# State-space stage of an audio tower: softplus per chunk, means and the cap of the inverse decays on GpSimd

## The reference, cut to what matters

```python
delta = minimum(softplus(x_ssm @ delta_W + delta_b), 0.5)
A_cont = -exp(A_log)                      # (128, 16): 16 states
DeltaA = delta[..., None] * A_cont
A_bar = clip(exp(DeltaA), 0, 1)
injection = expm1(DeltaA) / A_cont
B_cont = silu(x_ssm @ B_W + B_b)          # per state
B_cont = 0.5 * (B_cont - mean(B_cont, axis=(0, 1)))
B_bar = injection * B_cont
A_shift = concatenate([ones, A_bar[:, :-1]], axis=1)
pps = exp(cumsum(log(maximum(A_shift, 1e-6)), axis=1))
h_seq = cumsum(B_bar * pps, axis=1) / pps
C_coeff = silu(x_ssm @ C_W + C_b)
h_out = einsum('btdn,btdn->btd', h_seq, C_coeff)
```

## Time and profile before

| | |
|---|---|
| time, median of 3 runs | 969.38 us (968.5 to 972.45) |
| the profiled execution: time / span | 968.98 / 967.2 us |
| VectorE busy | 676.2 us (70%) |
| TensorE matmul busy | 668.2 us (69%) |
| ScalarE busy | 488.4 us (51%) |
| GpSimd busy | 288.5 us (30%) |
| granted TensorE clock, mean | 0.829 |

### The profile page before, as it was taken

How to read it: one execution, slowest core, us unless ns; L and a number is a source line. 1 busy time by engine, 2 the same in 40 slices (tenths; PEclk the granted TensorE clock), 3 DMA queues, 4 the chain that set the end, 5 groups by cost and what they waited for, 6 DMA issues and landing times.

```text
span 967.2 us, 10956 instructions
## 1 busy us (share of the span) xinstructions
PE 668.2 (69%) x2944; PEld 497.5 (51%) x2945; DVE 676.2 (70%) x1490; ACT 488.4 (51%) x691; POOL 288.5 (30%) x266
## 2 busy tenths in 40 slices
PE   6974353753744646666531996469999999999996
PEld 3542253753744646533430775236666566566564
DVE  0987279999999999987850442656767676676651
ACT  1234799888988888803320332224434344343531
POOL 0443101000000000002684343133644537354352
PEclk9995576876778768789655998779999999999999
DMA  4300424543453345307011121100000000000000
GB/s 156 121 25 0 161 76 85 109 79 73 84 106 81 62 97 101 63 0 267 19 28 32 51 61 43 53 1 0 1 9 8 1 9 1 9 1 8 8 1 16
DMA packets 22519, 50.91 MB, mean 53 GB/s; under 512 B 4610, under 2 KB 14827, under 8 KB 22128
## 3 DMA queue, kind: packets, MB, share of 16 engines
q0 software_dynamic: 6752, 24.53, 13.0%
q1 hardware_dynamic: 15728, 25.92, 8.6%
HBM read 24.41 MB, written 10.10 MB: 36 GB/s over the span
## 4 chain that ended last, share of the span: by engine, by line
DVE 38%; PE 32%; issue 11%; POOL 7%; ACT 5%; POOLq 2%; DMA 2%; DVEq 1%; ACTq 0%; SPq 0%
PE psum L1715 6%; DVE s_R L1053 5%; DVE s_R L1048 5%; DVE s_R L1058 5%; PE psum L1774 4%; PE psum L1477 3%; POOL s_R L676 3%; PE psum L1644 3%; PE psum L1657 2%; DVE s_R L1027 2%; POOLq L178 2%; DVE s_R L1032 2%; POOL x_sorted L620 1%; DVE s_stat L203 1%; PE psum L1650 1%
## 5 line engine op out<-in xcount | busy, mean ns | idle before, releaser
L1538 PE MATMUL psum<-s_xn_lo,s_split_hi 128*128 128x368 f32 x256 | 101.4, 396 | 146.1 <-ACT s_R L785 97.6
L1538 PEld LDWEIGHTS psum<-s_xn_lo,s_split_hi 128*128 128x128 f32 x256 | 60.3, 236 | 151.7 <-ACT s_R L785 100.1
L1715 PE MATMUL psum<-s_R 128*128 128x368 f32 (+1 forms) x288 | 107.6, 499 | 0.3
L881 ACT ACTIVATE s_R<-psum,s_cols 128x368 f32<-128x368 f32 x96 | 52.6, 567 | 104.3 <-PE psum L1709 104.0
L1053 DVE TENSOR_TENSOR_SCAN s_R<-s_R 128x2944 f32<-128x2944 f32 x16 | 100.7, 6291 | 0.6
L1539 PE MATMUL psum<-s_xn_hi,s_split_lo 128*128 128x368 f32 x256 | 98.3, 384 | 0.0
L605 POOL DMA_DIRECT2D s_xnfm<-s_R x14 | 17.1, 1218 | 271.3 <-DVEq L1062 271.3
L1540 PE MATMUL psum<-s_xn_hi,s_split_hi 128*128 128x368 f32 x256 | 97.6, 381 | 0.0
L1707 PE MATMUL psum<-s_xn_lo,s_split_hi 128*128 128x368 f32 x144 | 75.0, 521 | 1.3 <-ACT s_R L881 1.3
L1715 PEld LDWEIGHTS psum<-s_R 128*128 128x128 f32 (+1 forms) x288 | 54.9, 200 | 30.9 <-issue 3.5
L666 POOL TENSOR_TENSOR s_R<-s_R 128x368 f32<-128x368 f32 x48 | 45.4, 946 | 74.8 <-DVE s_R L1331 71.8
(11 more groups left out here) (221 smaller groups left out, 1591.8 us busy)
## 6 DMA issues: line engine op xcount, KB each, us to landing
s_xnfm<-s_R POOLq DMA_DIRECT2D x14, 1472.0 KB, 10.5
s_R<-in_xg SPq DMA_DIRECT2D x8, 744.0 KB, 4.2
x_sorted<-in_x_init SPq DMA_DIRECT2D x1, 5082.0 KB, 19.3
s_R<-in_w SPq DMA_DIRECT2D x2, 1536.0 KB, 9.3
s_wBC<-in_wBC SPq DMA_DIRECT2D x8, 256.0 KB, 2.9
s_R<-x_sorted SPq DMA_DIRECT2D x28, 66.0 KB, 1.8
s_R<-y_rows SPq DMA_DIRECT2D x8, 184.0 KB
out<-s_R SPq DMA_DIRECT2D x8, 184.0 KB
```

Source lines behind the costliest of these rows:

```text
L1538: pe.matmul(bank(c), w_hi[:, s, u, k, :], xn_lo[:, a:b], start=True, stop=False)
L1715: ins = pe.matmul(bank((2, 4)[e % 2]), w, fh[0:kk, e % 3, j], start=(j == 0), stop=(j == FT - 1))
```

## The change

- The argument of delta is cut at ln(e^0.5 - 1), so that its softplus is cut at 0.5; the pass of VectorE that cut the result is gone. ScalarE takes exponential and logarithm per chunk (softplus), in its loop over pairs of chunks, which is written out; the table that holds both functions is loaded at the start. The stage boundary between stages 1 and 2 is gone, and waits on x_split, delta_mm, delta_read and delta_act stand where it stood.
- The weights of the first pair are loaded, copied and split during stage 1.
- The mean of B is made by GpSimd in three small operations (mean_of), which raise mean_ready.
- The cap of ra and its zeros are made by GpSimd (cap), which raises ra_capped. The cap of state n waits for ra_ready and for th_free of state n - 1, which the drive of state n - 1 raises; the scan of n - 1 is VectorE's next instruction.
- GpSimd's order in a pair is: cap of the even state, add_state of the odd state before, mean of the even state, cap and mean of the odd state, add_state of the even state.
- In the first pair ScalarE takes the silus of state 0 before the decays of state 1. On VectorE w_lo is made between scan and read-out, and the read-out raises its semaphore itself.

```diff
         def stage_end(eng, k):
             eng.drain().then_inc(stage_done, 1)
-            eng.wait_ge(stage_done, 4 * k)
+            eng.wait_ge(stage_done, 4 * (k - 1))
...
             sp.dma_start(prio[:, :], t["prio"]).then_inc(wload, 16)
+            sp.dma_start(wBC[:, :, :, :], t["wBC"][0]).then_inc(wBC_ready, 16)
...
             split_x(NP - 1)
-            stage_end(pool, 1)
+            pool.wait_ge(x_split, NCH)
+            pool.wait_ge(delta_mm, NCH)
             pool.memset(Y[:, :], 0.0).then_inc(Y_zero, 1)
             pool.wait_ge(Y_zero, 1)
-            def add_state(n, u):
-                wait_apart(pool, prod_ready, n + 1)
+            def add_state(n, u, first=False):
+                wait_apart(pool, prod_ready, n + 3)
+                if not first:
+                    wait_apart(pool, Y_added, 16 * n)
                 pool.dma_start(Y[:, :], bufC[:, u], accum_op=ALU.add, max_dma_last_dim=TOK // 2 * 4)\
                     .then_inc(Y_added, 16)
-                pool.wait_ge(Y_added, 16 * n + 16)
+            def mean_of(n, u):
+                wait_apart(pool, bc_free, NH + (n * 2 + 1) * NH)
+                wait_apart(pool, th_free, n + 1)
+                step.add(pool.tensor_tensor(part[:, u, 0:2], part[:, u, 0:2], part[:, u, 2:4], ALU.add))
+                step.wait()
+                step.add(pool.tensor_tensor(mean[:, u:u + 1], part[:, u, 0:1], part[:, u, 1:2], ALU.add))
+                step.wait(True)
+                pool.tensor_scalar(mean[:, u:u + 1], mean[:, u:u + 1], 1.0 / TOK, 0.0, ALU.mult, ALU.add)\
+                    .then_inc(mean_ready, 1)
+            def cap(n, u, scan=True):
+                if scan:
+                    wait_apart(pool, th_free, n + 2)
+                wait_apart(pool, ra_ready, n + 1)
+                pool.tensor_scalar(ra[:, u], ra[:, u], 1e6, 0.0, ALU.min, ALU.max).then_inc(ra_capped, 1)
+                wait_apart(pool, ra_capped, 2 * n + 1)
+                pool.memset(ra[:, u, 0:TOK:L], 0.0).then_inc(ra_capped, 1)
+            cap(0, 0, False)
+            mean_of(0, 0)
+            cap(1, 1)
+            mean_of(1, 1)
+            add_state(0, 0, True)
+            for i in step.loop(NPAIR - 2, 2 * 2):
+                cap(i * 2 + 2, 0)
+                add_state(i * 2 + 1, 1)
+                mean_of(i * 2 + 2, 0)
+                cap(i * 2 + 3, 1)
+                mean_of(i * 2 + 3, 1)
+                add_state(i * 2 + 2, 0)
...
+            act.preload_act_table_set("natural_log_exp_and_others")
...
+            def softplus(i):
+                for u in range(2):
+                    c = i * 2 + u
+                    d = dl[:, 1 + c * CT:1 + c * CT + CT]
+                    act.wait_ge(delta_read, 2 + c + 1)
+                    act.activation(d, d, ACT.Exp).then_inc(delta_act, 1)
+                    act.wait_ge(delta_act, 2 * c + 1)
+                    act.activation(d, d, ACT.Ln, bias=1.0, scale=1.0).then_inc(delta_act, 1)
...
-            act.activation(dl[:, 1:1 + TOK], dl[:, 1:1 + TOK], ACT.Exp).then_inc(delta_act, 1)
-            act.wait_ge(delta_act, 1)
-            act.activation(dl[:, 1:1 + TOK], dl[:, 1:1 + TOK], ACT.Ln, bias=1.0, scale=1.0).then_inc(delta_act, 1)
-            stage_end(act, 1)
+            weights_hi(0, 0)
+            for i in range(NP):
+                if i + 1 < NP:
+                    bias_copy(i + 1)
+                normed_twice(i)
+                if i:
+                    softplus(i - 1)
+                norms_fm(i)
             act.sem_inc(bc_free, NH)
+            softplus(NP - 1)
+            load_table(ACT.Tanh, 0)
+            act.wait_ge(delta_act, 2 * NCH)
...
-            weights_hi(0, 0)
-            decays(0)
+            tanh(0, 0)
+            exp_minus(0)
+            exp_plus(0, 0)
+            silus(0, (0,), True)
+            exp_plus(1, 1)
+            tanh(1, 1)
+            exp_minus(1)
             weights_hi(1, 1)
-            silus(0, True)
+            silus(0, (1,), True)
...
-                step.add(dve.tensor_scalar(ra[:, u], ra[:, u], 1e6, None, ALU.min))
-                step.wait()
-                step.add(dve.memset(ra[:, u, 0:TOK:L], 0.0))
...
             def drive(n, u):
-                dve.wait_ge(bc_free, NH + (n * 2 + 1) * NH)
-                step.add(dve.reduce_sum(mean[:, u:u + 1], part[:, u, :], axis=AX))
-                step.wait()
-                step.add(dve.tensor_scalar(mean[:, u:u + 1], mean[:, u:u + 1], 1.0 / TOK, None, ALU.mult))
-                step.wait()
+                dve.wait_ge(ea_free, n + 2)
+                dve.wait_ge(mean_ready, n + 1)
                 dve.scalar_tensor_tensor(bufB[:, u], bufB[:, u], mean[:, u:u + 1], th[:, u],
                                          ALU.subtract, ALU.mult).then_inc(th_free, 1)
             def recur(n, u):
+                dve.wait_ge(ra_capped, 2 * n + 2)
                 dve.wait_ge(th_free, 2 + n + 1)
                 dve.tensor_tensor_scan(bufB[:, u], ra[:, u], bufB[:, u], 0.0, ALU.mult, ALU.add).then_inc(ra_free, 1)
...
                 drive(n, 0)
                 recur(n, 0)
-                read_out(n, 0)
                 if weights:
                     weights_lo(i + 1, s)
+                read_out(n, 0)
                 drive(n + 1, 1)
                 recur(n + 1, 1)
                 if more:
                     injection(n + 2, 0)
-                    decay(n + 2, 0)
                 read_out(n + 1, 1)
                 if more:
                     injection(n + 3, 1)
-                    decay(n + 3, 1)
```

More of the change, by code:

```diff
@@ L605, in add_state @@
                 pool.dma_start(Y[:, :], bufC[:, u], accum_op=ALU.add, max_dma_last_dim=TOK // 2 * 4)\
                     .then_inc(Y_added, 16)
-                pool.wait_ge(Y_added, 16 * n + 16)
-            with pool.Fori(0, NPAIR - 1) as i:
-                for u in range(2):
-                    add_state(i * 2 + u, u)
+            def mean_of(n, u):
[7 more added lines that the diff above has]
+                    .then_inc(mean_ready, 1)
@@ L612, in _ @@
+            add_state(0, 0, True)
[6 more added lines that the diff above has]
+                add_state(i * 2 + 2, 0)
+            cap(NS - 2, 0)
+            add_state(NS - 3, 1)
+            mean_of(NS - 2, 0)
+            cap(NS - 1, 1)
+            mean_of(NS - 1, 1)
             stage_end(pool, 2)
@@ L733, in _, with weights_hi @@
+            def weights_hi(i, s):
+                act.wait_ge(wBC_ready, 16 * i + 16)
+                act.activation(w_hi[:, s], wBC[:, :, :, :], ACT.Copy).then_inc(w_hi_ready, 1)
             act.sem_inc(nA.xs1_ready, 2)
             bias_copy(0)
-            with act.Fori(1, NP) as i:
-                bias_copy(i)
-                norms_fm(i - 1)
-            norms_fm(NP - 1)
-            act.wait_ge(delta_read, 2 + NCH)
-            act.activation(dl[:, 1:1 + TOK], dl[:, 1:1 + TOK], ACT.Exp).then_inc(delta_act, 1)
@@ L773, in group, with silus @@
                 return tile[:, u, h * HB * CT:(h + 1) * HB * CT].rearrange("p (s n) -> p s n", s=HB)
-            def weights_hi(i, s):
-                act.wait_ge(wBC_ready, 16 * i + 16)
-                act.activation(w_hi[:, s], wBC[:, :, :, :], ACT.Copy).then_inc(w_hi_ready, 1)
-            def silus(i, first=False):
-                for u in range(2):
+            def silus(i, us=(0, 1), first=False):
+                for u in us:
                     n = i * 2 + u
-                    act.wait_ge(B_free, n + 1)
+                    act.wait_ge(prod_ready, n + 1)
                     for h in range(NH):
@@ L1013, in _ @@
             delta_arg(NP - 1)
-            dve.wait_ge(delta_act, 2)
-            step.add(dve.tensor_scalar(dl[:, 1:1 + TOK], dl[:, 1:1 + TOK], 0.5, None, ALU.min))
-            stage_end(dve, 1)
             dve.sem_inc(th_free, 2)
@@ L1057, in read_out @@
                 dve.wait_ge(bc_free, NH + (n * 2 + 2) * NH)
-                step.add(dve.scalar_tensor_tensor(bufC[:, u], bufB[:, u], A_c[:, bass.ds(n, 1)], bufC[:, u],
-                                                  ALU.mult, ALU.mult))
-                step.wait()
-                dve.sem_inc(B_free, 1)
-                dve.sem_inc(prod_ready, 1)
+                dve.scalar_tensor_tensor(bufC[:, u], bufB[:, u], A_c[:, bass.ds(n, 1)], bufC[:, u],
+                                         ALU.mult, ALU.mult).then_inc(prod_ready, 1)
             def pair(i, s, more=True, weights=True):
@@ L1078, in pair @@
                     injection(n + 3, 1)
-                    decay(n + 3, 1)
-            dve.sem_inc(w_split, 1)
-            weights_lo(0, 0)
             injection(0, 0)
-            decay(0, 0)
-            decay(1, 1)
+            drive(0, 0)
+            recur(0, 0)
+            read_out(0, 0)
             injection(1, 1)
-            pair(0, 1)
-            for i in step.loop(NPAIR // 2 - 1, 2 * (2 * 2 + 2 * 3)):
+            weights_lo(1, 1)
+            drive(1, 1)
+            recur(1, 1)
+            injection(2, 0)
```

(15 more changed lines are left out.)

55 lines of the change are left out of this document (28 added, 27 removed).

## The result

The changed kernel takes 978.44 us, median of 7 runs (973.89 to 980.46), beside 969.99 us for the kernel before (7 runs): a ratio of 1.008, interval 1.0059 to 1.0101. It is slower by 0.8%, where 986 was forecast, and a span of 978.6 us was profiled, in a run of 980.46 us.

What follows compares the result with a forecast made beforehand. VectorE was taken to bound the states' stage. To the profiled 968.98 us came +26 for seven pairs at +3.7 each and -9 for the earlier start, giving 986, with a range of 942 to 1008.

Steps and rivals of the forecast that it cites:

- The main step: States' stage: the scan, as one more two-input instruction, excludes the cap on GpSimd; +3.7 us a pair, +26 us in all.
- the memset of Y costed at nothing: Start of the stage: this memset on an idle GpSimd only writes, so it was put at no cost.
- a GpSimd instruction waits for a whole run of VectorE's, not for one: States' stage: the even cap waits out injection, read-out and injection to 9.7 us, then runs to 12.7.
- The even half: From odd scan to even scan: the drive starts at 15.0 us instead of 14.0 and ends at 18.3.
- The odd half: Even scan to odd scan: cap and zeroing 3.2, mean 0.8 behind the read-out; odd drive ends at 35.9 us.
- 4 us of idle: Sign that the forecast is right: VectorE idle this long before the odd drive, released by GpSimd's mean.
- The start: Softplus per chunk and no stage boundary: scan of state 1 at 140.8 against 150.82, 10 us ahead; -9 us net.
- ScalarE's late entry into the next pair: After the first pair: ScalarE comes late to the next one, which costs about 1 us.
- The first: Rival: the scan doesn't exclude GpSimd, or GpSimd slips in; 36.0 us a pair, 944 us; chance 0.28.
- The second: Rival: the cap costs like a two-input operation, +62 us, 1048; chance of a cap above 4.5 us 0.08.
- The third: Rival: exclusion, but caps fall partly in VectorE's waits, about half of the 3.7 us remains; 973 or 969; chance 0.09.
- The break-even of 39.5 us a pair: States' stage: a pair under this length, 38.2 + 9 / 7, makes the changed kernel faster than before.

Runs made afterwards that it cites:

- the fill: The changed kernel with GpSimd's cap replaced by a memset of 1.0 that only writes, at the same place with the same waits: 945.77 us.
- the last section: The changed kernel with long-fulfilled waits put between VectorE's seven products in the attention's stage, beside GpSimd's small power: 981.09 us.
- the best version: The changed kernel with the cap and the means both back on VectorE: 953.03 us, ratio 0.9829 to the kernel before.

## Why the prediction was right and wrong

**Right.** VectorE bounded the stage; without a cap the pair falls to 35.7 us (22.2 + 13.54), where 35.4 to 36 was worked out. The main step, that the scan is one more instruction that excludes a GpSimd read, holds: the cap of 8.48 us over a scan of 6.29, and the fill that isn't held. It was taken from differences and products and is now shown for the scan, beside which the cap, which reads, holds VectorE for 2.4 us and the fill, which only writes, doesn't (945.77 us). That it hangs on the two inputs of VectorE's instruction was the author's estimate: no run varies them beside the cap, and the last section has an instruction with one input that kept GpSimd out too. That a GpSimd instruction which only writes costs VectorE nothing stands behind the memset of Y costed at nothing, and no row shows it; the fill of 2.56 us beside the scan does. The memset and the first weight load moved at no cost that the timelines show.

**Wrong, by three steps, the first of them in the mechanism.** The forecast was +17 us, the medians give +8.5.

- "a GpSimd instruction waits for a whole run of VectorE's, not for one", and from it the cap at 9.7 us. This step failed. In the states' stage the cap gets in at the end of the one instruction that is running: the even cap was to begin 9.7 us behind the odd scan's end and to be done at 12.7, and it was done 2.4 us behind it (190.40 against 187.97). The even half came out at 24.59, and the forecast's sum gives 24.6 for it (6.3 + 18.3), but that is luck, for it comes by another way: the cap holds the even injection, ScalarE's last exponential and all behind it come 2.4 us later, and zeroing and add_state lie in the shade.
- The odd half was put at 17.6 us (18.3 to 35.9) and is 16.34. The terms were cap and zeroing 3.2 and mean 0.8 behind the read-out. The hold is 2.4, it lies behind the scan so that the zeroing is over while VectorE works on, and of the mean only 0.5 us shows before the drive (idle 0.54, where 4 us of idle were named as a sign). That is 1.3 us a pair less than the sum before its overlaps of 0.3 were taken off. Seven pairs took 287.6 us against 7 x 41.9 = 293.3: 5.7 us.
- The start was put at 10 us, less 1 for ScalarE's late entry into the next pair. It is 12.7: ScalarE's last copy ended at 96.44 instead of the 98.0 of the sum, since ScalarE's last normalization in front of it began at 88.41, 1.1 us earlier than before (why is open), and the cap of state 1 ran beside the read-out of state 0 instead of behind the weights. The late entry cost 2.7 (the first even half is 27.26 us long, 138.08 to 165.34, against 24.59), which is in the 287.6.

**The rivals.** The first (scan not held, 944) is what the fill shows: it is the time of a cap that doesn't read. The second (a cap of 7.3 us) falls: where it goes first it takes 2.65 us, and 2.9 was taken. The third, caps that fall partly in VectorE's waits, is not what the changed kernel does, but with both caps first one of them does so, and the time was 960.39. The break-even of 39.5 us a pair agrees with the runs: 38.9 and 39.2 us (mean of seven) gave 962.92 and 966.07, 41.1 gave 978.44. They don't tell it from the 40.0 that the measured start gives (38.2 + 12.7 / 7).

The change loses since a cap of 1.69 us on the bounding engine was traded for one that stops that engine for 2.4 us, and more by where these fall. On VectorE both caps of a pair stand in the even half, where VectorE has 3.1 us of idle without them, so they cost 1.2 us a pair (36.9 with them, 35.7 without). The two holds of the changed kernel hit the head of ScalarE's chain and the odd half, which has no such idle, and cost 5.2 us a pair (40.93). Its other part, the start, is sound: in the best version, whose median is 17 us under the kernel before, the scan of state 1 is 14.6 us earlier (136.21, 150.82 before), and the seven pairs behind it are 4.0 us shorter (263.3, 267.3 before).

## What to carry to other kernels

Before an operation is moved to GpSimd because it is idle, look at what VectorE runs beside it: here the instructions that the cap held all read two tensors of SBUF, and the cap, which reads one, came back on VectorE with 2.4 of its 2.65 us. Such a move pays only if what comes back is less than VectorE's own time for the work (1.69 us for this cap) or falls where VectorE waits for another engine anyway. A fill, which only writes, cost at most 1.1 us in all there. When such a hold can't be avoided, choose by the release which instruction it hits: one that nobody waits for (here the odd injection) instead of the one at the head of ScalarE's chain was worth 12 us, and both caps first in GpSimd's list, so that the odd one's hold falls into VectorE's idle time, were worth 18.
